# Macaron block on eight cores: FFN weights transposed on TensorE instead of by DMA, XN copied out by ScalarE, PSUM banks split between gate and up

## Chip, cores and metric

The kernel runs as one program on the 8 cores of one Trainium2 chip. Each core has its own four sequences of the batch of 32 and its own copy of the weights; nothing is exchanged. The metric is device time in microseconds of the slowest core.

## What is computed

x has 32 sequences of 2048 tokens with 1024 features. Weights of the FFN come as int32 in -127..127.

```python
def ffn(x):
    gate = einsum('bsd,hd->bsh', x, w_gate / 127)   # hidden size 3072
    up   = einsum('bsd,hd->bsh', x, w_up / 127)
    return einsum('bsh,dh->bsd', silu(gate) * up, w_down / 127)

def attn(x):                                        # 16 heads of 64
    q, v  = x @ Wq.T, x @ Wv.T
    state = ema_scan(sigmoid(beta), v)              # state[t] = lam * state[t-1] + v[t]
    y     = layernorm(q * state) * ln_gamma + ln_beta
    return (y * silu(x @ Wg.T)) @ Wo.T

x = x + 0.5 * ffn(layernorm(x))
x = x + attn(layernorm(x))
x = x + 0.5 * ffn(layernorm(x))
```

## The kernel before

**Order of the work.** The kernel is recorded by a small class, `Em`: every call of `em.op`, `em.group` (a row of TensorE instructions) and `em.dma` appends an instruction to the list of its engine, and each engine runs its list strictly in the order in which the calls stand in the program. Waits follow from keys: `reads`, `writes` and `war` name pieces of buffers, and an instruction waits on semaphores for the last writer and, where it writes, for the readers. A DMA belongs to a stream with a semaphore of its own and waits for the one before it in its stream. A wait stands in the queue of the issuing engine, so everything behind it on that engine waits too. Streams "ns", "ts", "wl" and "tl" are all issued by SP (SyncE); "pc" (casts), "cl" (constants) and "io0" to "io3" (x in, result out) by GpSimd.

**Start.** GpSimd loads constants and a quarter of x, then `prep_cast` copies w_gate, w_up and w_down from int32 in HBM to bf16 in HBM (nat_g, nat_u, nat_d), then come the other three quarters of x and the casts of the four attention weights. SP transposes the FFN weights: `prep_T_gu` (L394) does w_gate and w_up in 8 slices each, a DMA transpose of 128 columns of nat into a half of SG (128 x 3072, L400) and a store of it to scr_g or scr_u (L405, pieces of 2 KB). `prep_T_d` (L407) does w_down in 24 slices of 128 x 1024, three by three (L416, L423). scr_g, scr_u and scr_d hold, in HBM, the weights with the contracted dimension on the partitions, in slabs of 1024 hidden units. Between these stand the loads of the first slab of scr_g into WA (L862) and of scr_u into WB (L866). SG is used again as the output of Silu in the FFN, so the first Silu waits for all users of SG in the preparation (`PREP_SG_KEYS`).

**Layer norm** (`layer_norm_to_xn`, L526). Per chunk of 128 tokens VectorE sums (L519) and ScalarE sums squares (L523); after small statistics VectorE subtracts the mean and scales (L544, into one of two halves of TMPTM), TensorE transposes eight blocks of 128 x 128 into the one bank PSB7b (L548), and VectorE copies the bank into XN, features on the partitions (L554). There are 12 layer norms of 16 chunks: three per sequence and core. The attention has a transposition of the same shape, L813, which ScalarE copies out (L817).

**FFN** (`ffn_phase`). Three slabs; in each, twice (hs) 16 groups of eight gate matmuls (L586), ScalarE's Silu into SG (L603), 16 groups of eight up matmuls (L613), VectorE's product into H (L623); then 32 groups of down matmuls (L638), added up in ACC (L648, L652). Gate and up groups go round the banks PSB0 to PSB3, down groups round PSB4 to PSB6. Weights are reloaded from scr for every slab into WA and WB.

**Attention** (`attn_phase`): projections (L696), the scan as matmuls with a matrix of decays (L732, L792), norm, gate and output projection (L824). The attention weights are transposed by DMA in `prep_T_attn` during the first FFN, in the halves of TSTB. The change leaves this as it is.

The parts that the diff touches:

Of the kernel before, what the change touches and what calls it, by code (L numbers as in the profile page):

```python
# [10 lines left out]
AF = mybir.ActivationFunctionType  # L11
# [6 lines left out]
D = 1024  # L18
HID = 3072
# [3 lines left out]
KC = D // 128  # L23
SLAB = 1024
# [222 lines left out]
def build_program():  # L247
# [4 lines left out]
    if DBG_TAPS:  # L252
# [13 lines left out]
        wdown=nc.dram_tensor("wdown", [D, HID], I32, kind="ExternalInput").ap(),  # L266
# [80 lines left out]
    for q in range(4):  # L347
# [24 lines left out]
    B_H = kVSC + kSTSB + kQC + kYC + kSGC  # L372
    B_ACC = ["WOT"] + kTYC + kY2C + kY2FM
    PREPC_KEYS = ["PREPC", "PREPC2", "PREPC3", "PREPC4", "PREPC5", "PREPC6"]
    PREP_SG_KEYS = (["tst0", "tst1"]
                    + [f"tst{a}_{i}" for a in range(2) for i in range(3)])
    WAR_ACC_B = ALL_ACC
    WAR_ACC_A = B_ACC + PREPC_KEYS

# [12 lines left out]
               writes=[f"nat_{tag}"])  # L392

    def prep_T_gu(tag, scr):  # L394
        if True:
            for kc in range(KC):
                slot = SG[:, (kc % 2) * HID:(kc % 2) * HID + HID]
                skey = f"tst{kc % 2}"
                em.dma("tl", lambda s, a=slot, b=nat[tag][:, 128 * kc:128 * (kc + 1)]:
                       s.dma_start(out=a, in_=b, transpose=True),  # L400
                       reads=[f"nat_{tag}"], writes=[skey],
                       war=ALL_SG + ["WGT"] + [f"tst{(kc % 2)}_{i}" for i in range(3)])
                dst = scr[:, :, kc, :]
                srcv = slot.rearrange("p (j h) -> p j h", h=SLAB)
                em.dma("ts", lambda s, a=dst, b=srcv: s.dma_start(out=a, in_=b),  # L405
                       reads=[skey], writes=[f"scrT_{tag}_{kc}"])
    def prep_T_d():  # L407
        for h0 in range(0, HID // 128, 3):
            half = (h0 // 3) % 2
            slot = SG[:, half * HID:half * HID + 3 * D]  # L410
            skey = f"tst{half}"
            for i in range(3):
                hc = h0 + i
                em.dma("tl", lambda s, a=slot[:, D * i:D * (i + 1)],
                       b=nat["wdown"][:, 128 * hc:128 * (hc + 1)]:
                       s.dma_start(out=a, in_=b, transpose=True),  # L416
                       reads=["nat_wdown"], writes=[f"{skey}_{i}"],
                       war=ALL_SG + ["WGT", skey])
            for i in range(3):
                hc = h0 + i  # L420
                dst = scr_d[:, hc // 8, hc % 8, :]
                em.dma("ts", lambda s, a=dst, b=slot[:, D * i:D * (i + 1)]:
                       s.dma_start(out=a, in_=b),  # L423
                       reads=[f"{skey}_{i}"], writes=[f"scrT_wdown_{hc}"])
# [101 lines left out]
    def layer_norm_to_xn(prestats=True):  # L526
        if not prestats:
            for c in range(NCH):
                ln_stats(c)
        em.op("vector", lambda v: v.tensor_scalar(  # L530
            stat("mu"), stat("ssum"), 1.0 / D, None, ALU.mult),
            reads=["ST_ssum"], writes=["ST_mu"])
        em.op("vector", lambda v: v.tensor_tensor(
            stat("musq"), stat("mu"), stat("mu"), ALU.mult),
            reads=["ST_mu"], writes=["ST_musq"])
        em.op("vector", lambda v: v.scalar_tensor_tensor(
            stat("var"), stat("ssq"), 1.0 / D, stat("musq"), ALU.mult, ALU.subtract),
            reads=["ST_ssq", "ST_musq"], writes=["ST_var"])
        emit_rsqrt(stat("var"), "ST_var", stat("sd"), "ST_sd",
                   stat("musq"), "ST_musq", stat("rstd"), "ST_rstd")  # L540
        for c in range(NCH):
            xc = X[:, D * c:D * (c + 1)]
            tm = TMPTM[:, D * (c % 2):D * (c % 2 + 1)]
            em.op("vector", lambda v, xc=xc, tm=tm, c=c: v.tensor_scalar(  # L544
                tm, xc, stat("mu", c), stat("rstd", c), ALU.subtract, ALU.mult),
                reads=[kX[c], "ST_mu", "ST_rstd"], writes=[f"TT{c % 2}"])
            bank, bkey = PSB7, "PSB7"
            items = [(lambda t, tm=tm, f=f, bank=bank: t.transpose(  # L548
                bank[:, 128 * f:128 * (f + 1)], tm[:, 128 * f:128 * (f + 1)], IDN[:]),
                [f"TT{c % 2}", "IDN"]) for f in range(KC)]  # L550
            em.group("tensor", items, writes=[bkey])
            xnv = XN[:].rearrange("p (f t) -> p f t", t=S)[:, :, 128 * c:128 * (c + 1)]
            bv = bank[:].rearrange("p (f t) -> p f t", t=128)
            em.op("vector", lambda v, xnv=xnv, bv=bv: v.tensor_copy(xnv, bv),  # L554
                  reads=[bkey], writes=[kXN[f][c] for f in range(KC)])

    def ffn_phase(tap=False, prestats=True, next_stats=True, tail_cb=None,
# [6 lines left out]
        for j in range(nsl):  # L564
# [5 lines left out]
            if not (skip_gw0 and j == 0):  # L570
                em.dma("wl", lambda s, a=wg_sl, j=j: s.dma_start(
                    out=a[:].rearrange("p (k h) -> p k h", h=SLAB), in_=scr_g[:, j]),
                    reads=[f"scrT_wgate_{kc}" for kc in range(KC)], writes=[wg_k])
                em.dma("wl", lambda s, a=wu_sl, j=j: s.dma_start(
                    out=a[:].rearrange("p (k h) -> p k h", h=SLAB), in_=scr_u[:, j]),
                    reads=[f"scrT_wup_{kc}" for kc in range(KC)], writes=[wu_k])
            if tap and j == 0:
                em.dma("st", lambda g, a=wg_sl: g.dma_start(out=dbg_wa, in_=a[:]),
                       reads=[wg_k], writes=["DBGWA"])
            for hs in range(2):  # L580
                for g in range(4):
                    for m4 in range(4):
                        m = 4 * hs + m4
                        bank = (g * 4 + m4) % 4
# [41 lines left out]
            if tap and j == 0:  # L626
# [3 lines left out]
                       reads=ALL_H, writes=["DBGH"])  # L630
            em.dma("wl", lambda s, a=wd_sl, j=j: s.dma_start(
                out=a[:].rearrange("p (k h) -> p k h", h=D), in_=scr_d[:, j]),
                reads=[f"scrT_wdown_{8 * j + i}" for i in range(8)], writes=[wd_k])
            for c in range(NCH):
                for n in range(2):
                    bank = 4 + (c * 2 + n) % 3
# [221 lines left out]
    for w in ("wq", "wv", "wgt", "wo"):  # L858
# [98 lines left out]
```

How the kernel before makes its waits and increments, by code:

```python
        def body(engobj, eng):  # L225
            waited = {}
            for inst in em.ins[eng]:
                for dep in inst["deps"]:
                    sem, val = resolve(dep)
                    key = id(sem)
                    if waited.get(key, 0) < val:
                        engobj.wait_ge(sem, val)
                        waited[key] = val
                bi = inst["fn"](engobj)
                if inst["stream"] is not None:
                    bi.then_inc(semh[("d", inst["stream"])], 16)
                elif inst["inc"]:
                    bi.then_inc(semh[("e", eng)], 1)
```

## Time and profile before

| | us |
|---|---|
| median of the two runs | 7146.09 |
| the two runs | 7094.26 and 7197.92 |
| profiled execution | 7077.24 |
| its span on the slowest core | 7075.6 |
| spans of the eight cores | 7030.7 to 7075.6 |
| TensorE, busy share of the span | 80% |
| VectorE, ScalarE, busy share | 30%, 18% |

The profile is of the slowest core, core 1. Engines are PE (TensorE matmul), PEld (its weight loads), DVE (VectorE), ACT (ScalarE), POOL (GpSimd) and SP. "Busy" leaves out the issuing of DMAs. A line number is that of the kernel before; in the changed kernel lines behind the preparation stand 22 further down (L586 is L608 there).

### The profile page before, as it was taken

Reading aid. Unit: us, or ns where it says so; the run is one execution under the profiler, and the core shown is the slowest. Engines: PE = TensorE matmul, PEld = TensorE weight load, DVE = VectorE, ACT = ScalarE, POOL = GpSimd, SP = SyncE. Lnnn points to the kernel's source line nnn. Section 1 sums busy time; section 2 is a strip of 40 time slices with the busy share of each in tenths; the row PEclk is TensorE's granted clock in tenths of the full one; section 3 lists DMA queues with packets and bytes.
Section 4 is the critical chain, followed back from the end, with each engine's and each line's share of the span. In section 5 each row is a group of like instructions: output and inputs, shape, how many; then the busy total and the mean of one; then the engine's idle time right before and its main releaser. Section 6 shows DMA issues by size and latency. Waiting matters only on the chain.

```text
span 7075.6 us, 78917 instructions; the slowest of 8 cores (7030.7 to 7075.6 us)
## 1 busy us (share of the span) xinstructions
PE 5637.5 (80%) x28562; PEld 2779.0 (39%) x28562; DVE 2151.0 (30%) x4049; ACT 1279.7 (18%) x2150; POOL 173.0 (2%) x112
## 2 busy tenths in 40 slices
PE   0007995877996998886996998885997899776999
PEld 0003443443442444443442444443443444443444
DVE  0201133443124125443124125344124224444123
ACT  1001111221211211221211211221211111222111
POOL 0000000000000000000000000000000000000000
PEclk9968997888997998887997998887998899887999
DMA  8961123000103001000013001000004000100002
GB/s 98 116 170 57 36 65 102 1 25 13 48 29 91 36 36 60 1 1 24 36 42 102 36 36 60 1 1 24 36 36 107 24 36 25 48 1 24 24 36 72
DMA packets 154435, 321.99 MB, mean 46 GB/s; under 512 B 112208, under 2 KB 112208, under 8 KB 141968
## 3 DMA queue, kind: packets, MB, share of 16 engines
q1 hardware_dynamic: 135936, 239.09, 11.0%
q0 software_dynamic: 18128, 77.84, 6.3%
q8 instruction: 246, 4.03, 0.2%
q14 instruction: 125, 1.02, 0.1%
HBM read 272.87 MB, written 88.08 MB: 51 GB/s over the span
## 4 chain that ended last, share of the span: by engine, by line
PE 70%; DVE 10%; DMA 7%; issue 5%; another core or an unknown queue 3%; SPq 2%; ACT 2%; DVEq 1%; ACTq 0%; POOL 0%; POOLq 0%
PE PSB L586 19%; PE PSB L613 18%; PE PSB L638 15%; PE PSB L696 10%; PE PSB L824 5%; PE PSB7b L548 2%; SPq L400 2%; DVE TMPTM L544 1%; DVE ACC L652 1%; DMA SG<-nat_g 1%; DMA X<-x 1%; ACT ACC L817 1%; PE PSB7b L813 1%; ACT TMPTM L761 1%
## 5 line engine op out<-in xcount | busy, mean ns | idle before, releaser
L623 DVE TENSOR_TENSOR H<-SG,PSB 128x512 bf16<-128x512 bf16 x768 | 528.3, 688 | 2868.8 <-PE PSB L613 2868.8
L586 PE MATMUL PSB<-XN,WA 128*128 128x512 bf16 x4096 | 908.6, 385 | 282.7 <-ACT SG L603 176.0
L638 PE MATMUL PSB<-WA,H 128*128 128x512 bf16 x4096 | 892.6, 380 | 32.6 <-DVE ACC L652 32.6
L603 ACT ACTIVATE SG<-PSB 128x512 bf16<-128x512 f32 x768 | 459.0, 598 | 2513.4 <-PE PSB L586 2513.4
L613 PE MATMUL PSB<-XN,WB 128*128 128x512 bf16 x4096 | 889.3, 379 | 0.0
L586 PEld LDWEIGHTS PSB<-XN,WA 128*128 128x128 bf16 x4096 | 405.4, 99 | 779.0 <-issue 308.7
L548 PE MATMUL PSB7b<-IDN,TMPTM 128*128 128x128 bf16 x1536 | 194.0, 306 | 640.0 <-DVE TMPTM L544 640.0
L638 PEld LDWEIGHTS PSB<-WA,H 128*128 128x128 bf16 x4096 | 401.6, 98 | 521.0 <-issue 42.0
L613 PEld LDWEIGHTS PSB<-XN,WB 128*128 128x128 bf16 x4096 | 400.7, 98 | 483.4
L652 DVE SCALAR_TENSOR_TENSOR ACC<-PSB,ACC 128x512 bf16<-128x512 f32 x512 | 352.4, 690 | 350.6 <-PE PSB L638 347.6
L613 PE MATMUL PSB<-XN,WA 128*128 128x512 bf16 x2048 | 444.6, 379 | 0.0
L586 PE MATMUL PSB<-XN,WB 128*128 128x512 bf16 x2048 | 444.6, 379 | 0.0
L638 PE MATMUL PSB<-WB,H 128*128 128x512 bf16 x2048 | 443.3, 379 | 0.0
L523 ACT ACTIVATE TMPTM<-X 128x1024 bf16<-128x1024 bf16 x192 | 203.0, 1058 | 1207.8 <-DMA X<-x 508.8
L824 PE MATMUL PSB<-ACC 128*128 128x512 bf16 x1024 | 350.5, 517 | 87.2 <-ACT ACC L817 87.2
L548 PEld LDWEIGHTS PSB7b<-IDN,TMPTM 128*128 128x128 bf16 x1536 | 148.3, 137 | 689.4 <-issue 689.4
L519 DVE TENSOR_REDUCE STATS<-X 128x1 f32<-128x1024 bf16 x192 | 234.2, 1220 | 273.0 <-DMA X<-x 254.1
L813 PE MATMUL PSB7b<-IDN,ACC 128*128 128x128 bf16 x512 | 64.1, 304 | 316.0 <-DVE ACC L809 316.0
L586 PEld LDWEIGHTS PSB<-XN,WB 128*128 128x128 bf16 x2048 | 200.4, 98 | 241.6
L638 PEld LDWEIGHTS PSB<-WB,H 128*128 128x128 bf16 x2048 | 200.4, 98 | 241.6
L613 PEld LDWEIGHTS PSB<-XN,WA 128*128 128x128 bf16 x2048 | 200.3, 98 | 241.7
L696 PE MATMUL PSB<-WB,XN 128*128 128x512 bf16 x1024 | 239.3, 388 | 38.6 <-DMA WB<-scr_wv 38.6
(89 smaller groups left out, 3549.9 us busy)
## 6 DMA issues: line engine op xcount, KB each, us to landing
WA<-scr_g SPq DMA_DIRECT2D x16, 2048.0 KB, 7.5
WB<-scr_u SPq DMA_DIRECT2D x16, 2048.0 KB, 7.5
WA<-scr_d SPq DMA_DIRECT2D x16, 2048.0 KB, 7.6
o<-X POOLq DMA_DIRECT2D x16, 2048.0 KB, 7.6
X<-x POOLq DMA_DIRECT2D x16, 1024.0 KB, 11.3
WB<-scr_g SPq DMA_DIRECT2D x8, 2048.0 KB, 7.4
WA<-scr_u SPq DMA_DIRECT2D x8, 2048.0 KB, 7.4
WB<-scr_d SPq DMA_DIRECT2D x8, 2048.0 KB, 7.4
```

The source lines that it names most:

```text
L400: s.dma_start(out=a, in_=b, transpose=True),
L519: em.op("vector", lambda v, xc=xc, c=c: v.reduce_sum(stat("ssum", c), xc, axis=AX.X), reads=[kX[c]], writes=["ST_ssum"])
L523: s.activation(sq, xc, AF.Square, accum_out=stat("ssq", c)),
L548: items = [(lambda t, tm=tm, f=f, bank=bank: t.transpose(bank[:, 128 * f:128 * (f + 1)], tm[:, 128 * f:128 * (f + 1)], IDN[:]), [f"TT{c % ...
L586: t.matmul(PSB[bank][:], wg_sl[:, SLAB * k + 128 * m:SLAB * k + 128 * (m + 1)], XN[:, S * k + 512 * g:S * k + 512 * (g + 1)], start=(k == ...
L603: s.activation(dst, PSB[bank][:], AF.Silu, scale=np32(1.0 / 127.0)),
L613: t.matmul(PSB[bank][:], wu_sl[:, SLAB * k + 128 * m:SLAB * k + 128 * (m + 1)], XN[:, S * k + 512 * g:S * k + 512 * (g + 1)], start=(k == ...
L623: v.tensor_tensor(dst, src0, PSB[bank][:], ALU.mult),
L638: t.matmul(PSB[bank][:], H[:, S * hc + 128 * c:S * hc + 128 * (c + 1)], wd_sl[:, D * hc + 512 * n:D * hc + 512 * (n + 1)], start=(hc == 0) ...
L652: v.scalar_tensor_tensor(dst, PSB[bank][:], SFIN, dst, ALU.mult, ALU.add),
L696: t.matmul(PSB[bank][:], XN[:, S * k + 128 * c:S * k + 128 * (c + 1)], wslot[:, D * k + 512 * n:D * k + 512 * (n + 1)], start=(k == 0), st ...
L824: t.matmul(PSB[bank2][:], Y2FM[sl][:, 128 * k:128 * (k + 1)], WOT[:, D * k + 512 * n:D * k + 512 * (n + 1)], start=(k == 0), stop=(k == KC ...
```

## The change

Three edits. First, the FFN weights are no longer transposed by DMA. For w_gate and w_up, 24 times each, SP loads 128 rows of nat into a half of TSTB, TensorE transposes eight blocks into PSB7b, VectorE copies the bank into one of two pieces of SG, and SP stores that to scr with a destination of 128 x 8 pieces of 128 values. For w_down, eight times, SP loads 128 rows of 3072 into SG, and three times eight blocks are transposed, copied and stored the same way. Each of these loads and stores has two streams that alternate, all issued by SP. Second, XN is copied out of PSB7b by ScalarE instead of VectorE. Third, gate groups use PSB0 and PSB1 and up groups PSB2 and PSB3, instead of both using all four.

```diff
     def prep_T_gu(tag, scr):
-            for kc in range(KC):
-                slot = SG[:, (kc % 2) * HID:(kc % 2) * HID + HID]
-                em.dma("tl", lambda s, a=slot, b=nat[tag][:, 128 * kc:128 * (kc + 1)]:
-                       s.dma_start(out=a, in_=b, transpose=True), ...
-                dst = scr[:, :, kc, :]
-                srcv = slot.rearrange("p (j h) -> p j h", h=SLAB)
-                em.dma("ts", lambda s, a=dst, b=srcv: s.dma_start(out=a, in_=b),
-                       reads=[skey], writes=[f"scrT_{tag}_{kc}"])
+        for r in range(HID // 128):
+            sl = r % 2
+            tk = f"tstb{sl}"
+            em.dma("nl" if sl == 0 else "nl2",
+                   lambda sy, a=TSTB[:, D * sl:D * (sl + 1)],
+                   b=nat[tag][128 * r:128 * (r + 1), :]: sy.dma_start(out=a, in_=b),
+                   reads=[f"nat_{tag}"], writes=[tk])
+            items = [(lambda t, sl=sl, kc=kc: t.transpose(
+                PSB7[:, 128 * kc:128 * (kc + 1)],
+                TSTB[:, D * sl + 128 * kc:D * sl + 128 * (kc + 1)], IDN[:]),
+                [tk, "IDN"]) for kc in range(KC)]
+            em.group("tensor", items, writes=["PSB7"])
+            ek = f"etmp{sl}"
+            em.op("vector", lambda v, sl=sl: v.tensor_copy(
+                SG[:, 1024 * sl:1024 * (sl + 1)], PSB7[:]),
+                reads=["PSB7"], writes=[ek], war=ALL_SG + ["WGT"])
+            dst = scr[:, r // 8, :, 128 * (r % 8):128 * (r % 8) + 128]
+            srcv = SG[:, 1024 * sl:1024 * (sl + 1)].rearrange("p (k q) -> p k q", q=128)
+            em.dma("tw" if sl == 0 else "tw2",
+                   lambda sy, a=dst, b=srcv: sy.dma_start(out=a, in_=b),
+                   reads=[ek], writes=[f"scrT_{tag}_r{r}"])
     def prep_T_d():
-        for h0 in range(0, HID // 128, 3):
...
+        for r in range(D // 128):
+            sl = r % 2
+            lk = f"sgw{sl}"
+            em.dma("nl" if sl == 0 else "nl2",
+                   lambda sy, a=SG[:, 3072 * sl:3072 * (sl + 1)],
+                   b=nat["wdown"][128 * r:128 * (r + 1), :]: sy.dma_start(out=a, in_=b),
+                   reads=["nat_wdown"], writes=[lk],
+                   war=ALL_SG + ["WGT", "etmp0", "etmp1"])
+            for sub in range(3):
+                ...
+                em.group("tensor", items, writes=["PSB7"])
+                esl = (r * 3 + sub) % 2
+                ek = f"etmpd{esl}"
+                em.op("vector", lambda v, esl=esl: v.tensor_copy(
+                    SG[:, 6144 + 1024 * esl:6144 + 1024 * (esl + 1)], PSB7[:]),
+                    reads=["PSB7"], writes=[ek], war=ALL_SG + ["WGT"])
+                dst = scr_d[:, sub, :, 128 * r:128 * (r + 1)]
+                ...
+                em.dma("tw" if esl == 0 else "tw2",
+                       lambda sy, a=dst, b=srcv: sy.dma_start(out=a, in_=b),
+                       reads=[ek], writes=[f"scrT_wdown_s{sub}r{r}"])
...
-            em.op("vector", lambda v, xnv=xnv, bv=bv: v.tensor_copy(xnv, bv),
+            em.op("scalar", lambda s, xnv=xnv, bv=bv: s.activation(xnv, bv, AF.Copy),
                   reads=[bkey], writes=[kXN[f][c] for f in range(KC)])
...
-                        bank = (g * 4 + m4) % 4        (gate)
+                        bank = (g * 4 + m4) % 2
...
-                        bank = (g * 4 + m4) % 4        (up)
+                        bank = 2 + (g * 4 + m4) % 2
```

SP's queue in the kernel before, at the end of w_gate and the beginning of w_up (nat_g and nat_u are the bf16 copies in HBM, scr_g and scr_u the transposed weights in HBM):

```order
L405 DMA scr_g<-SG 384x1x1024
L400 DMA_TRANSPOSE SG<-nat_g 128x3072
L405 DMA scr_g<-SG 384x1x1024
L862 DMA WA<-scr_g 128x8192
L400 DMA_TRANSPOSE SG<-nat_u 128x3072
L405 DMA scr_u<-SG 384x1x1024
```

The same place of SP's queue in the changed kernel:

```order
L417 DMA scr_g<-SG 128x8x128
L403 DMA TSTB<-nat_g 128x1024
L417 DMA scr_g<-SG 128x8x128
L884 DMA WA<-scr_g 128x8192
L403 DMA TSTB<-nat_u 128x1024
L417 DMA scr_u<-SG 128x8x128
```

Pairs of load and store take the place of pairs of transpose and store, 24 instead of 8 for each of the two weights, and each load stands behind the store of the slice before it.

VectorE's queue in the kernel before, from the constants to the first layer norm (a few rows of small statistics left out at the end):

```order
L478 TENSOR_TENSOR LBUF<-LBUF,ACC 128x128 x16
L519 TENSOR_REDUCE STATS<-X 128x1 x16
L530 TENSOR_SCALAR STATS<-STATS 128x16
L533 TENSOR_TENSOR STATS<-STATS 128x16
L536 SCALAR_TENSOR_TENSOR STATS<-STATS 128x16
```

VectorE's queue in the changed kernel at the same place:

```order
L500 TENSOR_TENSOR LBUF<-LBUF,ACC 128x128 x16
L411 COPY SG<-PSB7b 128x1024 x48
L438 COPY SG<-PSB7b 128x1024 x24
L541 TENSOR_REDUCE STATS<-X 128x1 x16
L552 TENSOR_SCALAR STATS<-STATS 128x16
```

All 72 copies of the preparation now stand ahead of the first layer norm on VectorE. On TensorE the transposes do the same; its queue before:

```order
L458 MATMUL PSB<-CROW,ACC 128x512 x2
L467 MATMUL PSB<-ACC 128x512 x4
L548 MATMUL PSB7b<-IDN,TMPTM 128x128 x128
L586 MATMUL PSB<-XN,WA 128x512 x128
L613 MATMUL PSB<-XN,WB 128x512 x128
```

and now:

```order
L480 MATMUL PSB<-CROW,ACC 128x512 x2
L489 MATMUL PSB<-ACC 128x512 x4
L405 MATMUL PSB7b<-IDN,TSTB 128x128 x384
L430 MATMUL PSB7b<-IDN,SG 128x128 x192
L570 MATMUL PSB7b<-IDN,TMPTM 128x128 x128
L608 MATMUL PSB<-XN,WA 128x512 x128
```

576 transposes of the preparation stand ahead of the first layer norm's 128 and of every FFN matmul.

## Rows read from the trace of the kernel before

**Rows 1.** The page: span, and two of its rows of 40 slices

```profile
span 7075.6 us, 78917 instructions; the slowest of 8 cores (7030.7 to 7075.6 us)
...
PE   0007995877996998886996998885997899776999
```

**Rows 2.** Waits up to 800 us: us in total, times, longest

```profile
ACT L603 <- DMA scr_d<-SG: 333.4, 1, 333.4
```

**Rows 3.** Timeline of TensorE at 396 us: start us, us, instruction

```profile
396.54 9.14 PE L586 MATMUL PSB<-XN,WA 128*128 128x512 bf16 x32 [106.74 <-DMA WA<-scr_g]
```

**Rows 4.** The chain of waits up to 900 us: start us, us, what

```profile
155.02 97.93 SPq L400
...
581.67 22.55 PE PSB L586 x96
604.22 27.63 PE PSB L613 x128
```

**Rows 5.** Timeline of GpSimd's queue up to 420 us

```profile
91.04 0.55 POOL L391 DMA_DIRECT2D nat_u<-wup  x1 [67.34 <-DMA nat_g<-wgate]
153.28 0.53 POOL L391 DMA_DIRECT2D nat_d<-wdown  x1 [61.69 <-DMA nat_u<-wup]
153.80 2.28 POOL L849 DMA_DIRECT2D X<-x  x3
...
303.11 0.50 POOL L391 DMA_DIRECT2D nat_wo<-wo  x1 [22.57 <-DMA nat_wgt<-wgt]
```

**Rows 6.** DMA queues from 100 to 145 us: packets, MB, share of 16 engines

```profile
q0 software_dynamic: 156, 5.11, 103.0%
q1 hardware_dynamic: 154, 0.04, 0.6%
```

**Rows 7.** DMA queues from 220 to 236 us

```profile
q0 software_dynamic: 1086, 2.16, 94.4%
q1 hardware_dynamic: 1089, 0.28, 13.6%
```

**Rows 8.** DMA issues of the whole execution: KB each, median us to landing

```profile
WA<-scr_g SPq DMA_DIRECT2D x16, 2048.0 KB, 7.5
...
scr_d<-SG SPq DMA_DIRECT2D x24, 256.0 KB, 2.6
...
nat_wo<-wo POOLq DMA_DIRECT2D x1, 2048.0 KB, 49.6
...
SG<-nat_d SPq DMA_TRANSPOSE x24, 3.5
```

**Rows 9.** DMA packets and SP's queue from 420 to 440 us

```profile
DMA packets 9100, 3.67 MB, mean 184 GB/s; under 512 B 8332, under 2 KB 8332, under 8 KB 9100
...
q1 hardware_dynamic: 9100, 3.67, 76.3%
```

**Rows 10.** Timeline of a layer norm's chunk at 1629 us

```profile
1629.35 1.01 PE L548 MATMUL PSB7b<-IDN,TMPTM 128*128 128x128 bf16 x8 [1.40 <-DVE TMPTM L544]
1630.46 0.69 DVE L554 COPY XN<-PSB7b 128x1024 bf16<-128x1024 bf16 x1 [1.26 <-PE PSB7b L548]
1631.07 0.54 DVE L544 TENSOR_SCALAR TMPTM<-X,STATS 128x1024 bf16<-128x1024 bf16 x1
```

**Rows 11.** Timeline of the first layer norm's statistics

```profile
241.22 5.19 DVE L519 TENSOR_REDUCE STATS<-X 128x1 f32<-128x1024 bf16 x4 [3.07 <-DMA X<-x]
...
251.57 0.55 DVE L544 TENSOR_SCALAR TMPTM<-X,STATS 128x1024 bf16<-128x1024 bf16 x1
```

**Rows 12.** Timeline of the attention's copy by ScalarE at 1607 us

```profile
1607.37 1.02 ACT L817 ACTIVATE ACC<-PSB7b 128x1024 bf16<-128x1024 bf16 x1 [8.91 <-PE PSB7b L813]
...
1608.54 5.55 PE L824 MATMUL PSB<-ACC 128*128 128x512 bf16 x16 [1.26 <-ACT ACC L817]
```

**Rows 13.** The chain of waits from 1000 us on: the first attention begins

```profile
1158.34 12.28 PE PSB L696 x48
```

**Rows 14.** Groups of the whole execution: busy us, mean ns, idle before

```profile
L623 DVE TENSOR_TENSOR H<-SG,PSB 128x512 bf16<-128x512 bf16 x768 | 528.3, 688 | 2868.8 <-PE PSB L613 2868.8
```

More of the change, by code:

```diff
@@ L353, in build_program @@
     em.stream("tl", "sync")
+    em.stream("nl", "sync")
+    em.stream("nl2", "sync")
+    em.stream("tw", "sync")
+    em.stream("tw2", "sync")
     kX = [f"X{c}" for c in range(NCH)]
@@ L374, in build_program @@
     PREPC_KEYS = ["PREPC", "PREPC2", "PREPC3", "PREPC4", "PREPC5", "PREPC6"]
-    PREP_SG_KEYS = (["tst0", "tst1"]
-                    + [f"tst{a}_{i}" for a in range(2) for i in range(3)])
+    PREP_SG_KEYS = (["etmp0", "etmp1", "sgw0", "sgw1", "etmpd0", "etmpd1"])
     WAR_ACC_B = ALL_ACC
@@ L407, in prep_T_d @@
-    def prep_T_d():
-        for h0 in range(0, HID // 128, 3):
[L409 to L424, printed above, removed]
+        for r in range(HID // 128):
[19 more added lines that the diff above has]
+                   reads=[ek], writes=[f"scrT_{tag}_r{r}"])
@@ new lines, in prep_T_d @@
+    def prep_T_d():
+        for r in range(D // 128):
[7 more added lines that the diff above has]
+            for sub in range(3):
+                items = [(lambda t, sl=sl, sub=sub, i=i: t.transpose(
+                    PSB7[:, 128 * i:128 * (i + 1)],
+                    SG[:, 3072 * sl + 1024 * sub + 128 * i:
+                         3072 * sl + 1024 * sub + 128 * (i + 1)], IDN[:]),
+                    [lk, "IDN"]) for i in range(8)]
+                em.group("tensor", items, writes=["PSB7"])
[5 more added lines that the diff above has]
+                dst = scr_d[:, sub, :, 128 * r:128 * (r + 1)]
+                srcv = SG[:, 6144 + 1024 * esl:6144 + 1024 * (esl + 1)].rearrange(
+                    "p (k q) -> p k q", q=128)
+                em.dma("tw" if esl == 0 else "tw2",
+                       lambda sy, a=dst, b=srcv: sy.dma_start(out=a, in_=b),
+                       reads=[ek], writes=[f"scrT_wdown_s{sub}r{r}"])
@@ L572, in ffn_phase @@
                     out=a[:].rearrange("p (k h) -> p k h", h=SLAB), in_=scr_g[:, j]),
-                    reads=[f"scrT_wgate_{kc}" for kc in range(KC)], writes=[wg_k])
+                    reads=[f"scrT_wgate_r{r}" for r in range(HID // 128)], writes=[wg_k])
                 em.dma("wl", lambda s, a=wu_sl, j=j: s.dma_start(
                     out=a[:].rearrange("p (k h) -> p k h", h=SLAB), in_=scr_u[:, j]),
-                    reads=[f"scrT_wup_{kc}" for kc in range(KC)], writes=[wu_k])
+                    reads=[f"scrT_wup_r{r}" for r in range(HID // 128)], writes=[wu_k])
             if tap and j == 0:
@@ L583, in ffn_phase @@
                         m = 4 * hs + m4
-                        bank = (g * 4 + m4) % 4
+                        bank = (g * 4 + m4) % 2
                         items = [(lambda t, k=k, m=m, g=g, wg_sl=wg_sl, bank=bank:
@@ L610, in ffn_phase @@
                         hc = m
-                        bank = (g * 4 + m4) % 4
+                        bank = 2 + (g * 4 + m4) % 2
                         items = [(lambda t, k=k, m=m, g=g, wu_sl=wu_sl, bank=bank:
@@ L632, in ffn_phase @@
                 out=a[:].rearrange("p (k h) -> p k h", h=D), in_=scr_d[:, j]),
-                reads=[f"scrT_wdown_{8 * j + i}" for i in range(8)], writes=[wd_k])
+                reads=[f"scrT_wdown_s{j}r{r}" for r in range(D // 128)], writes=[wd_k])
             for c in range(NCH):
@@ L863, in build_program @@
         out=WA[:].rearrange("p (k h) -> p k h", h=SLAB), in_=scr_g[:, 0]),
-        reads=[f"scrT_wgate_{kc}" for kc in range(KC)], writes=["WSLOTA"])
+        reads=[f"scrT_wgate_r{r}" for r in range(HID // 128)], writes=["WSLOTA"])
     prep_T_gu("wup", scr_u)
@@ L867, in build_program @@
         out=WB[:].rearrange("p (k h) -> p k h", h=SLAB), in_=scr_u[:, 0]),
-        reads=[f"scrT_wup_{kc}" for kc in range(KC)], writes=["WSLOTB"])
+        reads=[f"scrT_wup_r{r}" for r in range(HID // 128)], writes=["WSLOTB"])
     prep_T_d()
```

5 lines of the change are left out of this document (removed).

## Prediction

> **What bounds the kernel now.** I read the page from the top. The profiled execution took 7077 us for a span of 7075.6, and the page's slices (177 us each) show TensorE idle in the first three and busy at 0.8 to 0.9 in nearly all the others [rows 1]. So there are two regimes, a start of some 580 us and a matmul-bound rest, and every edit has to be priced in its own.
>
> In the start, the waits up to 800 us say what held the engines: ScalarE's first Silu waited 333 us for the store of w_down's last transposed slice [rows 2]. The gate matmuls had been ready at 396.5 and TensorE did four groups (32 matmuls) [rows 3], but SG is the buffer of the prepared weights as well, Silu writes it, and with four banks full TensorE stopped. The chain of waits shows the start as DMA alone (an early transpose of w_gate holds SP for 98 us), then steady matmuls from 581.7 and 27.63 us for 128 of them, or 216 ns each [rows 4]. Less the 32 matmuls already done (6.9 us), the old start ends at an equivalent of 574.8.
>
> Why the early transposes are slow decides this case. GpSimd's queue issues the casts of the weights one behind the other: w_up at 91 when w_gate's is done, w_down at 153, then the rest of x, then the four attention weights, the last at 303 [rows 5]. Between 100 and 145 the cast queue moved 156 packets of 32 KB (5.11 MB in all) at a DMA share of 1.03 and the SP queue 154 packets of 256 B: one for one [rows 6]. A cast packet lasts 45 us x 16 engines / 156 = 4.6 us. So whatever SP has in flight moves one packet per DMA engine each 4.6 us, however small the packet. While x is loaded the ratio is again one for one, at 1089 packets of each kind in 16 us, or 0.24 us a pair [rows 7]. The cost on SP is counted in packets, not in bytes.
>
> **The change, part by part.**
>
> A. The new preparation. For w_gate and w_up 48 steps: SP loads 128 rows (128 pieces of 2 KB, 8 per DMA engine), TensorE transposes eight blocks into PSB7, VectorE copies them out, SP stores 128 x 8 pieces of 256 B, 64 per DMA engine. SP runs in order and the next load is issued behind the store, which waits for the copy, so the steps are a chain. One step costs 72 packets per DMA engine. w_down is 8 loads of 128 x 6 KB and 24 such stores.
>
> A1, beside the casts. A cast of 6 MB gives each engine 12 packets, so a store gets 12 of its 64 pieces there, and the rest only in the gap before the next cast. That makes one step per cast: one at 91 to 97, one with the gap behind w_up, about one and a half with x (72 x 0.24 = 17 us each), and one each for wq, wv, wgt and wo. I count 7 steps by 342 us; the last cast is issued at 303, its predecessor of the same size took 22.6 us [rows 5] and it took 49.6 itself [rows 8], so the casts end between 326 and 352.
>
> A2, the 41 steps behind the casts. A store of 128 pieces of 2 KB lands 2.6 us after its issue [rows 8]; at about 0.1 us a piece, 8 per engine are 0.8 us, and 1.8 us are start and receipt. The pieces of 256 B to HBM are shown nowhere. Nearest: w_down's transposes, which read 1024 rows of 256 B, 64 per engine, land after 3.5 us, so (3.5 - 1.8)/64 = 27 ns a piece [rows 8]. The lower end is 20 ns: from 420 to 440 the 16 engines were busy for 0.763 x 320 us with 9100 packets, 8332 of them small and 768 of 2 KB at 0.1 us [rows 9], which leaves 167 us / 8332. The upper end is the full price of a 2 KB piece, which a load of scr_g bounds: 8 pieces of 16 KB per engine in 7.5 - 1.8 us [rows 8] are 0.09 us per 2 KB, and I round up to 0.1. I take 40 ns, nearer to the transposes, and above them because those pieces are read from HBM and these written to it. The step is then 1.8 + 64 x 0.04 = 2.6 for the store ahead in the queue + 0.8 for the load + 1.12 from first transpose to copy + 0.69 for the copy [rows 10] + 0.4 of hand-overs = 7.4 us. 41 x 7.4 = 303, so 645.
>
> The Trainium skill (DMA: Bandwidth & Descriptors, Specifications) says that transfers below 512 B are done as a read-modify-write. No row here shows such a store. By that rule a piece costs about twice the transposes' 27 ns, 54 ns, which adds some 37 us in A2 and 20 in A4 to the forecast; the sum here goes by 40.
>
> A3. Between w_gate, w_up and w_down stand two loads of 2 MB in SP's queue, 7.5 us each [rows 8] and 1.5 for the landing of the store ahead: 18, so 663.
>
> A4. w_down, per block of 128 rows: the last store ahead and the load 1.8 + 2.6 + 2.3 (8 pieces of 6 KB at 0.29), transposes and copy 2.0, then two more of 2.9 each (a store waits for the one two before it): 14.5, times 8 is 116, so the preparation ends at 779.
>
> B. The first layer norm is no longer hidden. In program order its VectorE part and its transposes now stand behind all 72 preparation copies; before, they ran around 250 us under the casts. Its price: 16 sums at 5.19 us per four = 20.8, the small statistics, from the end of the last sums at 241.22 + 5.19 to the first scaling at 251.57, 5.1 [rows 11], then 16 chunks at 2.3 (part C) + 0.6 = 37.4. Together 63, so the first FFN matmul at 842, against 575: +267 us. The wait that Silu had for SG is over by then.
>
> C. XN's copy on ScalarE, in 12 layer norms. A chunk took 2.41 us: 1.11 from TensorE's start to the copy's, 0.61 to the next scaling, which stands behind the copy in VectorE's queue, 0.54 for it and 0.15 until TensorE starts again [rows 10]. Now the scaling runs under TensorE and the period is 1.12 + ScalarE's copy + 0.15. That copy, of the same 128 x 1024 from the same bank in the attention, takes 1.02, and TensorE starts 0.15 behind it [rows 12]: 2.30, or 0.11 us saved per chunk. It counts in 10 of the 12: the first is in B, and the second ends behind the transposes of the attention weights, which hold TensorE until 1158 [rows 13]. 10 x 16 x 0.11 = -18 us. Bounds: if VectorE's 0.69 held on ScalarE too, -70; if the strided XN write made it 1.3, +27. I take the row of the same shape.
>
> D. Two banks for gate and two for up instead of four. A group takes 8 x 216 ns = 1.73 us, its eviction at most 0.69 (the product; Silu is shorter) [rows 14]. With two banks the eviction must be over one group later, and it is a full microsecond early. 128 matmuls take 27.63 us, their bare sum, so no group waits for a bank now and there is nothing to win: 0. The bound above is a late first eviction at the head of each FFN, when two groups instead of four can be ahead: a microsecond or two, eight times.
>
> Sum: +267 - 18 = +249 on 7077, so 7326. The two runs shown lie at 7094 and 7198, their median 69 above the profiled execution, the lower 17 above it. I add the 17: **7345 us**.
>
> **Rivals.**
>
> R1, the small pieces cost what 2 KB pieces cost (0.1 us). Drain 6.2 instead of 2.6 us; steps 11 us, w_down's block 25. 41 x 3.6 = 148, 8 x 10.5 = 84 and some 20 in A1 on top of the forecast: 7597. For it: the record of a DMA packet is partly fixed cost. Against it: 27 ns for the reads.
>
> R2, the small pieces are as cheap as the cheapest row (20 ns) and the step needs only some 5.5 us. 41 steps are 226 us, w_down 84 to 104, so the FFN starts at 730 to 765 and the time is 7231 to 7266. For it: transposes do run so. Against it: reads. It ends about at the 2% bound (7289 against the median of 7146), which is what a measurement of this kernel can tell from no change.
>
> R3, faster: SP is not held by the casts. The only traffic seen beside them was transposes and stores of 2 KB, at one packet per cast packet; if plain loads and stores of many pieces went in bundles, the 48 steps would start at 91; at 5.2 us each (the step with pieces at their cheapest) the FFN begins at 91 + 250 + 18 + 90 + 63 = 512 against 575, and with part C the time is 7077 + 17 - 63 - 18 = 7013 us. It decides at 42 steps done by 352, 6.2 us each; the one-for-one count of rows 6 and the 98 us of rows 4 speak against it.
>
> R4, the change doesn't show: the start shortens nothing and costs nothing because the casts, not the preparation, set it. They end at 352 at the latest, and only 223 us are left for 41 steps, w_down and the layer norm; less the 63 of the norm that is 2.5 us a store. Time 7075 to 7095.
>
> **How the numbers follow.** Forecast and its surroundings (7270 to 7480) 0.6, R1 0.15, R2 0.17, R3 0.04, R4 0.04. The range reaches from R2's low part to R1: 7215 to 7600. Slower by over 2% needs 7289: all of R1 (0.15), nearly all of the forecast's (0.57), a quarter of R2 (0.04): 0.76. Within 2%: 0.20. Faster: 0.04.
>
> **What would show it.** Right: first L608 matmul at 800 to 880; 6 to 8 stores of scr_g issued by 345; stores of scr_u 7 to 8 us apart; the waits show SP waiting for VectorE's copies and TensorE in the start for loads of TSTB; the 16 chunks of later layer norms 2.3 apart; attention and FFN stages of equal length. Wrong: stores 11 us apart (R1) or under 6 (R2), many steps inside the casts (R3), FFN groups over 1.73 us with TensorE waiting for Silu (D), or a span that grew anywhere behind the first FFN.

## Result, and the profile after

| | kernel before | changed kernel |
|---|---|---|
| executions that are compared, us | 7067 to 7118 | 7255 to 7268 |
| ratio, 95% interval | | 1.024 (1.020 to 1.028) |
| mean span of a core, us | 7056 | 7250 |
| median of all executions of the comparison, us | 7453 | 7611 |

The change makes the kernel slower by 2.4%, some 190 us. The forecast was slower, by 3.5%, with 7345 us and a range of 7215 to 7600. In over half of the executions of either kernel, the profiled one of the changed kernel among them, one die or both ran with a lower granted clock, which lifts the medians of the last row by some 350 us; every comparison of times below leaves those dies out. Effects of a few us are read from the third row's quantity, the mean span of the four cores of a die; it scatters by 4 to 9 us between dies. It is written "die mean" below.

The rows of the changed kernel are of core 1 and from the start, where the clock was granted in full (PEclk 1.00 up to 700 us) and hardly any matmuls run.

The DMA queues from 100 to 145 us, core 1, packets, MB and share of the 16 engines (against [rows 6]), and from 345 to 420 us, behind the casts:

```profile
q0 software_dynamic: 145, 4.75, 99.5%
q1 hardware_dynamic: 143, 0.04, 0.6%
...
DMA packets 14328, 6.35 MB, mean 85 GB/s; under 512 B 12790, under 2 KB 12790, under 8 KB 14326
...
q1 hardware_dynamic: 14326, 6.32, 34.4%
...
scr_g<-SG SPq DMA_DIRECT2D x13, 256.0 KB, 2.8
TSTB<-nat_g SPq DMA_DIRECT2D x13, 256.0 KB, 3.2
```

Beside w_up's cast the stores of 256 B pieces move one packet per cast packet, just as the transposes did. Behind the casts 13 loads and 13 stores pass in 75 us, the 16 engines are busy for a third of it, and a store of 1024 small pieces lands in 2.8 us, 0.2 later than the old ones of 128 large pieces [rows 8]. The busy time of 0.344 x 1200 = 413 us, less 1536 large packets at the 0.09 to 0.1 us that the prediction had for one, leaves 20 to 22 ns for each of the 12790 small pieces; 21 is used below.

The chain of waits of core 1 up to 1000 us (start, us, what), which answers to [rows 4]:

```profile
93.92 61.36 another core or an unknown queue
156.68 74.60 another core or an unknown queue
234.10 24.06 DMA TSTB<-nat_g
261.00 17.52 DMA TSTB<-nat_g
...
301.99 17.88 DMA TSTB<-nat_g
322.69 3.33 DMA TSTB<-nat_g
328.84 3.04 DMA TSTB<-nat_g
...
576.78 2.57 DMA scr_u<-SG
...
670.94 5.46 DMA SG<-nat_d
...
683.89 1.23 DVE STATS L541
```

The first two rows are the times in which a load stands behind a store in SP's ring while a cast runs. Until 320 us there is a step per cast (20 us apart for the small ones), and from 322.69 on a load each 6.0 us (the sixteenth behind it is issued at 419.47), with 3.1 us of it the load's own flight. The preparation ends at 683, and the first layer norm begins there.

One step of w_up, and one chunk of the first layer norm, in the timeline of core 1:

```profile
449.60 0.69 DVE L411 COPY SG<-PSB7b 128x1024 bf16<-128x1024 bf16 x1 [5.28 <-PE PSB7b L405]
450.38 0.37 SPq L417 DMA_DIRECT2D scr_u<-SG  x1
450.90 0.47 SPq L403 DMA_DIRECT2D TSTB<-nat_u  x1
...
454.40 1.01 PE L405 MATMUL PSB7b<-IDN,TSTB 128*128 128x128 bf16 x8 [4.98 <-DMA TSTB<-nat_u]
455.59 0.69 DVE L411 COPY SG<-PSB7b 128x1024 bf16<-128x1024 bf16 x1 [5.29 <-PE PSB7b L405]
```

```profile
713.09 1.02 ACT L576 ACTIVATE XN<-PSB7b 128x1024 bf16<-128x1024 bf16 x1 [1.46 <-PE PSB7b L570]
713.17 0.55 DVE L566 TENSOR_SCALAR TMPTM<-X,STATS 128x1024 bf16<-128x1024 bf16 x1 [1.94 <-PE PSB7b L570]
...
714.47 1.01 PE L570 MATMUL PSB7b<-IDN,TMPTM 128*128 128x128 bf16 x8 [1.48 <-ACT XN L576]
715.57 1.02 ACT L576 ACTIVATE XN<-PSB7b 128x1024 bf16<-128x1024 bf16 x1 [1.46 <-PE PSB7b L570]
```

In the step nothing overlaps: load, transposes, copy, store, and then the next load is issued. In the chunk VectorE's scaling does run under TensorE, as foreseen, but ScalarE ends at 714.11 and TensorE starts at 714.47, 0.36 us later and not 0.15. The chunk takes 2.48 us against 2.41 before [rows 10].

The waits up to 900 us and the head of the first FFN (timeline) of core 1:

```profile
PE PSB7b L405 <- DMA TSTB<-nat_g: 354.9, 24, 74.9
PE PSB7b L405 <- DMA TSTB<-nat_u: 127.3, 24, 12.1
...
PE PSB L608 <- ACT SG L625: 0.6, 1, 0.6
```

```profile
747.60 4.75 PE L608 MATMUL PSB<-XN,WA 128*128 128x512 bf16 x16
```

TensorE waits for loads, and at the head of the FFN 0.6 us for Silu. The FFN begins at 747.6; in the kernel before, core 1 began it at 581.7 [rows 4] with 32 matmuls done. Core 1 was the latest of its program in that start: on core 2 the chain of waits of the kernel before has steady matmuls from 553.62, and over the eight cores they begin at 551.5 to 581.7, 561 in the mean. In the changed kernel the first FFN matmuls of the eight cores lie within 8 us.

```profile
553.62 6.32 PE PSB L586 x18
```

### The profile page after: what moved, and what is told of

It reads as the page before. It is cut to its first block, busy times and chain, and to the rows that moved or that the text cites. A ratio compares the mean times of both kernels' runs of the same rounds, so it can differ in the third digit from the quotient of the medians.

```text
span 7830.1 us, 81015 instructions; the slowest of 8 cores (7333.1 to 7830.1 us)
## 1 busy us (share of the span) xinstructions
PE 6327.1 (81%) x29138; PEld 3000.2 (38%) x29138; DVE 2102.7 (27%) x3929; ACT 1476.9 (19%) x2342; POOL 173.1 (2%) x112
## 4 chain that ended last, share of the span: by engine, by line
PE 73%; DVE 8%; DMA 7%; issue 4%; ACT 4%; another core or an unknown queue 3%; DVEq 0%; SPq 0%; ACTq 0%; POOL 0%; POOLq 0%
PE PSB L608 19%; PE PSB L635 19%; PE PSB L660 16%; PE PSB L718 9%; PE PSB L846 5%; PE PSB7b L570 2%; ACT XN L576 2%; DMA TSTB<-nat_g 2%; DMA TSTB<-nat_u 1%; DVE STATS L541 1%; DMA X<-x 1%; ACT ACC L839 1%; DMA o<-X 1%; ACT TMPTM L783 1%
## 5 line engine op out<-in xcount | busy, mean ns | idle before, releaser
L608 PE MATMUL PSB<-XN,WA 128*128 128x512 bf16 x4096 | 1018.0, 417 | 0.6 <-ACT SG L625 0.6
L660 PE MATMUL PSB<-WA,H 128*128 128x512 bf16 x4096 | 1002.2, 413 | 18.7 <-DVE ACC L674 18.7
L635 PE MATMUL PSB<-XN,WB 128*128 128x512 bf16 x4096 | 1004.9, 414 | 0.0
L660 PEld LDWEIGHTS PSB<-WA,H 128*128 128x128 bf16 x4096 | 427.2, 104 | 591.1 <-issue 388.2
L608 PEld LDWEIGHTS PSB<-XN,WA 128*128 128x128 bf16 x4096 | 431.0, 105 | 579.9 <-issue 395.9
L635 PEld LDWEIGHTS PSB<-XN,WB 128*128 128x128 bf16 x4096 | 427.7, 104 | 571.8 <-issue 379.4
L635 PE MATMUL PSB<-XN,WA 128*128 128x512 bf16 x2048 | 503.0, 414 | 0.0
L608 PE MATMUL PSB<-XN,WB 128*128 128x512 bf16 x2048 | 501.1, 413 | 0.0
L660 PE MATMUL PSB<-WB,H 128*128 128x512 bf16 x2048 | 499.5, 413 | 0.0
L846 PE MATMUL PSB<-ACC 128*128 128x512 bf16 x1024 | 366.9, 537 | 87.4 <-ACT ACC L839 87.4
L405 PE MATMUL PSB7b<-IDN,TSTB 128*128 128x128 bf16 x384 | 48.6, 307 | 479.7 <-DMA TSTB<-nat_g 351.7
L576 ACT ACTIVATE XN<-PSB7b 128x1024 bf16<-128x1024 bf16 x192 | 196.4, 1023 | 814.5 <-PE PSB7b L570 814.5
L635 PEld LDWEIGHTS PSB<-XN,WA 128*128 128x128 bf16 x2048 | 213.9, 104 | 286.2 <-issue 191.0
L608 PEld LDWEIGHTS PSB<-XN,WB 128*128 128x128 bf16 x2048 | 213.6, 104 | 284.8 <-issue 185.6
```

The source lines that it names most:

```text
L576: em.op("scalar", lambda s, xnv=xnv, bv=bv: s.activation(xnv, bv, AF.Copy), reads=[bkey], writes=[kXN[f][c] for f in range(KC)])
L608: t.matmul(PSB[bank][:], wg_sl[:, SLAB * k + 128 * m:SLAB * k + 128 * (m + 1)], XN[:, S * k + 512 * g:S * k + 512 * (g + 1)], start=(k == ...
L635: t.matmul(PSB[bank][:], wu_sl[:, SLAB * k + 128 * m:SLAB * k + 128 * (m + 1)], XN[:, S * k + 512 * g:S * k + 512 * (g + 1)], start=(k == ...
L660: t.matmul(PSB[bank][:], H[:, S * hc + 128 * c:S * hc + 128 * (c + 1)], wd_sl[:, D * hc + 512 * n:D * hc + 512 * (n + 1)], start=(hc == 0) ...
L846: t.matmul(PSB[bank2][:], Y2FM[sl][:, 128 * k:128 * (k + 1)], WOT[:, D * k + 512 * n:D * k + 512 * (n + 1)], start=(k == 0), stop=(k == KC ...
```

## Experiments

**The three edits apart.** Each edit alone, in the kernel before or with the others undone.

The new preparation alone:

```diff
 # the changed kernel with
-            em.op("scalar", lambda s, xnv=xnv, bv=bv: s.activation(xnv, bv, AF.Copy),
+            em.op("vector", lambda v, xnv=xnv, bv=bv: v.tensor_copy(xnv, bv),
-                        bank = (g * 4 + m4) % 2
+                        bank = (g * 4 + m4) % 4
-                        bank = 2 + (g * 4 + m4) % 2
+                        bank = (g * 4 + m4) % 4
```

> Only the new preparation (XN's copy back on VectorE, four banks again). Theory 1, the new preparation and the first layer norm behind it are the whole loss: the first FFN matmul of steady work at about 745 us and the time 165 to 185 us above the kernel before. Theory 2, part of the loss comes from the copy on ScalarE or from the banks: less than 150 us above it.

Measured: 7250 to 7253, ratio 1.0235 (1.019 to 1.028); die mean 7241, 185 above the kernel before and 9 below the changed one. The FFN begins at 738.6 on core 2, in its chain of waits:

```profile
738.63 11.53 PE PSB L608 x49
```

The preparation with the layer norm behind it is the loss, 185 of 194 us. It is all there when the first attention begins, 185 us later on core 2 (TensorE's timeline of the kernel before, then of this one), and the two spans of core 2 differ by 182:

```profile
1129.80 2.77 PE L696 MATMUL PSB<-WB,XN 128*128 128x512 bf16 x6 [37.44 <-DMA WB<-scr_wv]
...
1314.87 2.34 PE L718 MATMUL PSB<-WB,XN 128*128 128x512 bf16 x5 [32.30 <-DMA WB<-scr_wv]
```

The copy on ScalarE alone:

```diff
 # the kernel before with
-            em.op("vector", lambda v, xnv=xnv, bv=bv: v.tensor_copy(xnv, bv),
+            em.op("scalar", lambda s, xnv=xnv, bv=bv: s.activation(xnv, bv, AF.Copy),
```

> The kernel before with XN's copy on ScalarE. By the trace of the changed kernel a chunk of a layer norm takes 2.49 us instead of 2.41: 10 exposed layer norms x 16 x 0.08 = 13 us slower. By the prediction, with 0.15 us from the copy to the next transposes, it would be 18 us faster.

Measured: 7080 and 7089; die mean 7062, 6 above the kernel before, within the scatter. The changed kernel lies 9 above the run before this one, which differs by this copy and the banks. So the copy is a loss of 6 to 9 us, hardly clear of the scatter, and not the gain of 18. The groups of this run show what happened (core 2; busy us, mean ns, idle before and its releasers):

```profile
L554 ACT ACTIVATE XN<-PSB7b 128x1024 bf16<-128x1024 bf16 x192 | 196.4, 1023 | 353.0 <-PE PSB7b L548 353.0
...
L548 PE MATMUL PSB7b<-IDN,TMPTM 128*128 128x128 bf16 x1536 | 194.1, 305 | 656.3 <-DVE TMPTM L544 388.1 <-ACT XN L554 268.3
```

TensorE's idle time ahead of the transposes is 656 us in 12 layer norms, and was 648 on the same core with the copy on VectorE; the difference is in the releasers. From the copy's start to TensorE's next start it was 0.61 + 0.54 + 0.15 = 1.30 us with the scaling in between [rows 10], and is 1.02 + 0.36 = 1.38 with ScalarE's longer copy and its longer hand-over.

The banks alone:

```diff
 # the kernel before with, for gate and for up
-                        bank = (g * 4 + m4) % 4
+                        bank = (g * 4 + m4) % 2
-                        bank = (g * 4 + m4) % 4
+                        bank = 2 + (g * 4 + m4) % 2
```

> The kernel before with two banks for gate and two for up. Theory: within 5 us, no group waits for a bank. Rival: the first Silu behind a layer norm is late and TensorE waits at each head of an FFN, 5 to 20 us slower. In the start only two groups instead of four can be done before Silu may write SG: 16 matmuls or 3.5 us later in any case.

Measured: ratio 0.9999 (0.996 to 1.004), die mean 7 above the kernel before with a scatter of 10. Nothing that can be told from none; in its trace gate groups wait for Silu once, for 173.3 us in the start, as before (171.7, both on core 2).

**The price of a small piece.**

```diff
 # the changed kernel with
-            dst = scr[:, r // 8, :, 128 * (r % 8):128 * (r % 8) + 128]
-            srcv = SG[...].rearrange("p (k q) -> p k q", q=128)
+            dst = scr[:, r // 8, r % 8, :]
+            srcv = SG[...]
 # and the same for scr_d
```

> The changed kernel, whose preparation stores the same bytes in pieces of 2 KB per partition (the weights then lie wrongly in HBM, so the output is not the reference's). If a small piece costs 40 ns or is a read-modify-write at 54, a step shrinks by 64 x 0.04 - 0.8 = 1.8 us or more, and 41 steps and 24 stores of w_down by over 100 us. If it costs 20 ns, the drain is 1.3 against 0.8 us, a step shrinks by 0.5 us at most and the time by 20 to 35 us, beside the 9 steps under the casts, which gain more because 8 packets pass a cast where 64 don't: 20 to 80 us there.

Measured: 7233, die mean 7221, 29 below the changed kernel. The DMAs from 345 to 420 us on core 5:

```profile
q1 hardware_dynamic: 3690, 8.03, 32.1%
...
scr_g<-SG SPq DMA_DIRECT2D x13, 256.0 KB, 2.0
TSTB<-nat_g SPq DMA_DIRECT2D x12, 256.0 KB, 2.7
```

Stores land 0.8 us sooner and loads 0.5, a step takes 5.5 us instead of 6.0. The 29 us are within the 20 to 35 for a piece of 20 ns; a piece of 40 ns would have given over 100 us. The Trainium skill (DMA: Bandwidth & Descriptors, Specifications) has transfers below 512 B done as a read-modify-write, from which the prediction estimated 54 ns a piece; the runs show 21. In this kernel stores of 256 B to HBM cost about what the transposes' pieces of that size do. It is no cheap form, since 1024 of them take some 1.7 times the engine time of 128 pieces of 2 KB (1024 x 0.021 = 21 us against 128 x 0.1 = 13), but the step is not bound by the DMA engines, which are busy for a third of it.

The larger gain expected under the casts did not come: by 325 us core 1 has issued eight stores instead of seven, and core 5 eight in both kernels. The queues of core 2 from 100 to 145 us show that SP's packets are counted there whatever their size, 144 to 144, now nearly all of 2 KB (0.26 MB, where 143 packets had been 0.04):

```profile
q0 software_dynamic: 144, 4.72, 96.7%
q1 hardware_dynamic: 144, 0.26, 1.8%
```

The count is not one for one under every cast: from 260 to 276 us, beside a cast of 2 MB, core 5 of this run moved 64 cast packets and 32 of SP. Why was not looked into.

**The casts.** The four attention weights are cast behind the preparation, once in the changed kernel and once in the kernel before.

```diff
-    for w in ("wq", "wv", "wgt", "wo"):
-        prep_cast(w)
     build_consts()
...
     prep_T_d()
+    for w in ("wq", "wv", "wgt", "wo"):
+        prep_cast(w, after=["scrT_wdown_s2r7"])     # before: ["scrT_wdown_23"]
```

> The changed kernel with the four attention weights cast behind the preparation of w_down instead of before it. Theory, a cast holds SP's packets at one per cast packet: the changed kernel's steps go 18 to 24 us apart from 234 to 320 us and 6.0 apart behind that; without the four casts four steps come 15 us earlier each, so the start ends 40 to 60 us earlier and the time is 7205 to 7225 (the changed kernel: 7255 to 7267). Rival, a step's time is its own in the early stretch too: no change.

Measured: 7191, die mean 7181, 69 below the changed kernel. The chain of waits on core 2 has loads 6 us apart from 232 us on, where they were 20 apart until 322:

```profile
222.88 6.85 DMA TSTB<-nat_g
232.56 3.01 DMA TSTB<-nat_g
238.39 3.00 DMA TSTB<-nat_g
```

> The kernel before with the same move of the four casts. Theory: its transposes of w_gate took 37, 22, 30 and 11 us under these casts and 7 behind them, so 60 to 85 us go: 6990 to 7020 (the kernel before: 7067 to 7106). Rival, the start is bound by the transposes' own rate: under 15 us.

Measured: 6983 and 6987, ratio 0.986 (0.983 to 0.989), die mean 83 below. The transposes of w_gate take 7 us from 251 on (chain of waits, core 2):

```profile
251.41 7.00 DMA SG<-nat_g
...
259.10 7.11 DMA SG<-nat_g
```

A cast on GpSimd's queue is what holds SP's packets, in either kernel. The gain of 69 us is above the 40 to 60 that were expected, that of 83 at the upper end of 60 to 85.

**The chain of a step.**

```diff
 # the changed kernel, w_gate and w_up; w_down the same way
+        load(0)
         for r in range(HID // 128):
+            if r + 1 < HID // 128:
+                load(r + 1)              # ahead of the store of r
...
-            em.dma("nl" if sl == 0 else "nl2", ...)
```

> The changed kernel with each load of the preparation issued one step ahead, before the store that waits for the copy. Theory, a step of 6.0 us is a chain (load 3.2, transposes 1.1, copy 0.7, issue): with the load taken out of it a step is 3 us, 41 steps give 120 us and w_down's blocks 8 x 4 = 35, so 7100 to 7120. Rival, the DMA engines or SP set the step's time: under 30 us.

Measured: 7105 to 7114, ratio to the kernel before 1.003 (1.002 to 1.005), die mean 155 below the changed kernel. Copies and transposes in the timeline of core 2:

```profile
401.98 1.01 PE L410 MATMUL PSB7b<-IDN,TSTB 128*128 128x128 bf16 x8 [1.96 <-DMA TSTB<-nat_u]
403.52 0.69 DVE L416 COPY SG<-PSB7b 128x1024 bf16<-128x1024 bf16 x1 [2.63 <-PE PSB7b L410]
...
404.99 1.01 PE L410 MATMUL PSB7b<-IDN,TSTB 128*128 128x128 bf16 x8 [2.00 <-DMA TSTB<-nat_u]
```

A step is 3.0 us. The order of loads and stores in SP's queue was worth 155 us, four fifths of the change's loss.

**The layer norm in the start.**

```diff
 # the changed kernel: after the store of each step r
+    def hook_g(r):                        # in w_gate's steps
+        if 6 <= r < 22: ln_stats(r - 6)
+        if r == 22:     ln_head()
+    def hook_u(r):                        # in w_up's steps
+        if r < NCH:     ln_chunk(r)
```

> The changed kernel with the first layer norm spread over the steps of the preparation (sums beside w_gate's steps, chunks beside w_up's) and nothing else. Theory: the 62 us of the layer norm behind the preparation go, and 16 chunks, which share PSB7b with a step, lengthen w_up's steps by up to 1 us: 45 to 62 us less, 7200 to 7215. Rival: TensorE and VectorE serve the chunks in the chain of the steps at their full 2.5 us: then only 20 us are gained.

Measured: 7196, die mean 7183, 67 below the changed kernel. One of w_up's steps with its chunk, core 5:

```profile
479.96 0.69 DVE L414 COPY SG<-PSB7b 128x1024 bf16<-128x1024 bf16 x1 [5.37 <-PE PSB7b L408]
...
481.25 1.01 PE L585 MATMUL PSB7b<-IDN,TMPTM 128*128 128x128 bf16 x8 [1.47 <-DVE TMPTM L581]
...
482.36 1.02 ACT L591 ACTIVATE XN<-PSB7b 128x1024 bf16<-128x1024 bf16 x1 [5.49 <-PE PSB7b L585]
484.61 1.01 PE L408 MATMUL PSB7b<-IDN,TSTB 128*128 128x128 bf16 x8 [2.35 <-DMA TSTB<-nat_u]
485.80 0.69 DVE L414 COPY SG<-PSB7b 128x1024 bf16<-128x1024 bf16 x1 [4.69 <-PE PSB7b L408]
```

TensorE is done with the chunk at 482.26 and ScalarE at 483.38, both before the load has landed and the next step's transposes start at 484.61, and the step is 5.84 us, no longer than without it. The layer norm behind the preparation cost all it took, 65 us on core 1 (682.6 to 747.6).

All three together:

> All three: loads one step ahead, the attention casts late, and the first layer norm spread over the steps of the preparation (sums beside w_gate's steps, chunks beside w_up's). Theory: 155 us by the loads ahead, 55 by the layer norm, 50 by the casts, so about 7000, 60 to 90 below the kernel before. Rival, the chunks lengthen each step by their own 2.5 us since they share the bank PSB7b: then the layer norm gives back only 15 and the time is 7040.

Measured: die mean 6999 (three dies of three executions; there is no whole execution to compare), 56 below the kernel before. The three gains add up to 291 apart and to 251 together. With the load ahead, a step of 3.0 us no longer has room for a chunk, and w_up's steps with a chunk come 4.9 us apart (timeline of core 2):

```profile
350.66 1.01 PE L410 MATMUL PSB7b<-IDN,TSTB 128*128 128x128 bf16 x8 [1.37 <-ACT XN L595]
353.14 1.01 PE L589 MATMUL PSB7b<-IDN,TMPTM 128*128 128x128 bf16 x8 [1.47 <-DVE TMPTM L585]
355.52 1.01 PE L410 MATMUL PSB7b<-IDN,TSTB 128*128 128x128 bf16 x8 [1.37 <-ACT XN L595]
```

TensorE's transposes of the step now wait for the chunk's copy out of the bank that both use. The rival thus held for the bank, 16 x 1.9 = 30 of the missing 40 us. That the time still came out at the theory's 7000 is partly luck: the terms for the layer norm and the casts had been taken too low, by 12 and 19 us.

**A version that beats both.** The kernel before, with late casts and its transposes one ahead.

```diff
 # the kernel before with late casts, w_gate and w_up
+        trans(0)
         for kc in range(KC):
+            if kc + 1 < KC:
+                trans(kc + 1)            # streams "tl", "tl2" in turn
             em.dma("ts" if kc % 2 == 0 else "ts2", ...)
 # w_down: the three transposes of the next group, one ahead of each store
```

> The kernel before with the attention casts late, and its DMA transposes issued one ahead (for w_down three ahead) on two alternating streams, so that stores and landings lie under the next transpose. With the late casts alone the stretch from 242 to 484 us is 16 transposes 7.6 apart, two loads and 24 slices of w_down 4.7 apart. Theory, this is start and landing more than packets: 5.5 and 2.5 us each, the start 70 to 90 us shorter, 6900 to 6920. Rival, the transposes' own packet rate (192 pieces of 256 B per engine, 27 ns each = 5.2 us and 1.7) is the bound together with the stores' 2.4: no more than 30 us gained.

Measured: 6927 to 6934; die mean 6918, 138 below the kernel before (2.0%) and 55 below the late casts alone, between the 70 to 90 of the theory and the 30 of the rival. The gain is in w_down only: its 24 slices go from 358 to 421 us, 2.6 us each, where they took 4.8. The steps of w_gate and w_up are no shorter, at 8.2 us against 7.6 (chain of waits, core 2):

```profile
322.79 3.50 SPq L401
326.38 4.54 DMA scr_u<-SG
330.99 3.40 SPq L401
334.48 4.53 DMA scr_u<-SG
```

SP is held at L401 for 3.4 us while it issues a transpose of 3072 rows, and each store now stands behind that transpose in the ring and lands 4.5 us after its issue. The next transpose writes the half of SG which that store reads, and waits for it, so the two times add up. For those 16 the rival's number held, no gain, but its reason was not shown: the 16 engines were busy for 79% from 300 to 345 us, not all the time. Beside w_down's transposes (370 to 418 us) they were busy throughout.

## Why the prediction was right and where it failed

**Right.** The sign and the place: all but 6 to 9 us of the loss is in the start, made of a chain of steps, casts that hold it, and a layer norm that came out of its cover. That beside w_up's cast one SP packet passes per cast packet was read from the old trace; it held for the new stores of 256 B and for pieces of 2 KB, and two runs with the casts moved gained 69 and 83 us. The layer norm of part B was put at 63 us; moved under the preparation it gave 67. Part D's nothing was nothing. R3, that the new loads and stores slip past the casts, is refuted by the rows from 100 to 145 us. R4, that the casts alone set the start, is refuted by the chain of waits: the last cast had landed by 319 us and the preparation ran on to 683, in steps of 6.0 us and blocks of 12.4.

Of the signs that it had named for being right, most did not come: the first L608 matmul is at 748 and not from 800 on, ten stores of scr_g were issued by 345 and not 6 to 8, stores of scr_u lie 6.0 us apart and not 7 to 8, and chunks of the layer norm 2.48 and not 2.3.

**The term that failed is A2, the price of a 256 B piece and with it the step's time.** The prediction had 27 ns from its nearest row, 20 as a lower end, and took 40 because these pieces are written. They cost 21. A step took 6.0 us instead of 7.4: 41 x 1.4 = 57 us too much. Within it, 64 pieces at 0.019 us less are 1.2 us. The load was put at 1.8 + 2.6 + 0.8 = 5.2 us with the drain of the store ahead, and landed after 3.2, so 0.8 are left besides the piece; with stores of 2 KB the same sum gives 3.4 where 2.7 was measured, and why the parts don't simply add up was not tried. Against this, hand-overs and the issue of the store took 1.0 us and not 0.4.

The same piece is in A4, where a block of w_down took 12.4 us (from 596.44 to 670.94, six blocks) instead of 14.5, another 17. A1 counted seven steps by 342 us; they were done by 320, which makes 22 more: the last cast took 20.5 us where the prediction had 49.6 from core 1 of the old trace, the longest of the eight (under 25 on five of them; the three with 35 to 50 are the cores that began their FFN last). Together that is 96 us of the start, where 842 was foreseen and 748 measured on core 1. R2, with pieces at 20 ns and the FFN from 730 to 765, was the case that came true: it had 7231 to 7266 us, and 7255 to 7268 were measured. It had been given 0.17.

**Part C had the wrong sign.** It took 0.15 us from the end of ScalarE's copy to TensorE's next start, from the attention's copy. In the layer norm it is 0.36, so a chunk went from 2.41 to 2.48 instead of 2.30: 10 x 16 x 0.07 = 11 us lost by this working (6 to 9 measured) where 18 were to be gained. One difference is that the layer norm's first transpose waits for two engines, VectorE's scaling and ScalarE's copy, where the old kernel had both on one engine; whether that second wait is the 0.2 us was not tried.

**The reference point, and luck.** The old start was taken as 574.8 us from core 1. That core was some 28 us later into its FFN than core 2, yet its whole span was only 20 longer than the die means. In the mean of the eight cores the old start ends at 561 less the 6.9 of the 32 matmuls already done, and the new one at 746: 192 us, near the 194 of the die means, where core 1 of the two profiles has only 747.6 - 574.8 = 173. So the forecast's 267 had 94 too much in the new start, gave 20 of that back by the reference, and part C's wrong sign took off another 27. That 3.5% came as near to 2.4% as it did is partly luck. The last sum is also off by 2 us, 7326 + 17 being 7343, which changes nothing.

## What to carry to other kernels

Before a preparation stage is priced, write down its issuing queue in order: a load that stands behind a store that waits for a copy makes a chain of flights, and here issuing the load first was worth 155 us while storing in large pieces gave 29. Whatever is emitted later in program order on the same engines, such as the first layer norm, is no longer hidden; count it whole. Where a large cast on another queue shares the DMA engines, count packets rather than bytes, as the 144 to 144 here, and move transfers that nobody needs yet behind the ones on the path. Take the durations and the reference from more than one core: here the core that the page showed was the latest of eight in both.

## What was not expected of the hardware

- A store of 1024 pieces of 256 B to HBM took 21 ns a piece of engine time and landed in 2.8 us; 128 pieces of 2 KB landed in 2.0 in the same place. The two differ in engine time by less than a factor of two.
- ScalarE's copy of 128 x 1024 from PSUM took the same 1.02 us with a strided destination in the layer norm as in the attention with a contiguous one, but TensorE's start behind it came 0.36 us later instead of 0.15.
- Beside w_up's cast SP moved one packet per cast packet, whether of 256 B (143 to 145) or nearly all of 2 KB (144 to 144).
- DMA transposes of 3072 rows issued one ahead gained nothing (8.2 us a step against 7.6), each waiting for the store of the half of SG that it writes; those of 1024 rows nearly halved their time (2.6 against 4.8).
